# A decoder layer on one core: cross maximum subtracted by VectorE, one exp a block, and a new order of the scores

## What is computed

```python
def reference(x, ctx, w_qkv, b_qkv, w_proj, b_proj, w_q, w_k, w_v, w_o, k0, k1, k2, s0, s1, s2):
    x = layernorm(x + self_attention(x, w_qkv, b_qkv, w_proj, b_proj))     # causal
    # cross-attention
    q, k, v = heads(x @ w_q), heads(ctx @ w_k), heads(ctx @ w_v)
    attn = softmax(einsum('bhqd,bhkd->bhqk', q, k) * 64 ** -0.5)
    x = layernorm(x + merge(einsum('bhqk,bhkd->bhqd', attn, v)) @ w_o)
    h = relu(s0 * dense(k0, concatenate([x, -x]))) * 2
    h = relu(s1 * dense(k1, h)) * 2
    return layernorm(x + s2 * dense(k2, h))
```

## Time and profile before

| | |
|---|---|
| median of 3 runs | 2832.47 us (2832.13 to 2832.97) |
| the profiled execution | 2829.64 us, its span 2827.6 us |
| TensorE matmul busy | 2296.6 us (81% of the span) |
| VectorE busy | 1710.5 us (60%) |
| ScalarE busy | 1150.0 us (41%) |
| GpSimd busy | 720.4 us (25%) |
| mean granted clock of TensorE | 0.941 |

### The profile page before, as it was taken

How to read it: one execution, slowest core, us unless ns; L and a number is a source line. 1 busy time by engine, 2 the same in 40 slices (tenths; PEclk the granted TensorE clock), 3 DMA queues, 4 the chain that set the end, 5 groups by cost and what they waited for, 6 DMA issues and landing times. The chain is left out here.

```text
span 2827.6 us, 54422 instructions
## 1 busy us (share of the span) xinstructions
PE 2296.6 (81%) x18572; PEld 1931.4 (68%) x18572; DVE 1710.5 (60%) x4548; ACT 1150.0 (41%) x2568; POOL 720.4 (25%) x847
## 2 busy tenths in 40 slices
PE   8994688888888788888878788888878788888877
PEld 6883576766676666766667677766667666766666
DVE  4542566666666666666665566666665666666664
ACT  5552344443344334443344334444344334444332
POOL 1000222322322322232232322232232322232231
PEclk9996899999999999999999999999999999999999
DMA  8984322333321332333331232333332232233310
GB/s 265 293 265 95 52 41 51 60 60 60 56 55 46 52 56 34 60 60 60 60 56 48 46 56 34 60 60 60 60 56 47 47 56 38 55 60 60 60 31 12
DMA packets 205155, 196.57 MB, mean 70 GB/s; under 512 B 50130, under 2 KB 184306, under 8 KB 205042
## 3 DMA queue, kind: packets, MB, share of 16 engines
q1 hardware_dynamic: 205108, 195.94, 32.7%
HBM read 69.37 MB, written 58.87 MB: 45 GB/s over the span
## 5 line engine op out<-in xcount | busy, mean ns | idle before, releaser
L1180 PE MATMUL ps<-r_h,w 128*128 128x256 f16 x2048 | 511.6, 289 | 2.1 <-DVE r_l L806 2.0
L1181 PE MATMUL ps<-r_l,w 128*128 128x256 f16 x2048 | 508.9, 288 | 0.0
L821 DVE CUSTOM_DVE_ANT_0 junk<-ps,causal 128x128 bf16<-128x128 f32 (+1 forms) x1024 | 322.8, 353 | 196.5 <-PE ps L1212 188.4
L488 POOL TENSOR_TENSOR p<-p,inv 128x308 f32<-128x308 f32 x256 | 228.4, 899 | 612.1 <-DVE inv L872 612.1
L623 ACT ACTIVATE probs<-ps 128x768 f32<-128x768 f32 x256 | 207.7, 813 | 295.2 <-PE ps L1223 294.4
L598 ACT ACTIVATE p<-ps,low 128x77 f32<-128x77 f32 x1024 | 268.0, 409 | 97.0 <-DVE low L860 94.2
L1318 PE MATMUL ps<-vo_h,p2t 128*128 128x256 f32 (+1 forms) x1280 | 241.9, 291 | 50.9 <-DVE p2t L879 49.2
L475 POOL TENSOR_SCALAR_AFFINE_SELECT probs<-probs 128x512 f32<-128x512 f32 x256 | 164.1, 641 | 430.8 <-ACT probs L623 430.6
L806 DVE SCALAR_TENSOR_TENSOR r_l<-ps,r_h 128x512 f16<-128x512 f32 x256 | 175.7, 687 | 135.8 <-ACT r_h L563 135.7
L1180 PEld LDWEIGHTS ps<-r_h,w 128*128 128x128 f16 x2048 | 211.4, 103 | 55.7 <-issue 20.7
L1223 PE MATMUL ps<-q_st,k_bd 128*128 128x256 f32 x1024 | 180.8, 306 | 74.6 <-DMA q_st<-neg_max 61.0
(11 more groups left out here) (145 smaller groups left out, 5027.3 us busy)
## 6 DMA issues: line engine op xcount, KB each, us to landing
vo_scratch<-vo_out SPq DMA_DIRECT2D x80, 448.0 KB, 4.3
vo<-vo_scratch SPq DMA_DIRECT2D x64, 512.0 KB
q_st<-p2t SPq DMA_DIRECT2D x192, 128.0 KB
k_bd<-p2t SPq DMA_DIRECT2D x192, 128.0 KB, 6.6
q<-q SPq DMA_DIRECT2D x128, 128.0 KB, 2.1
k_bd<-k_scratch SPq DMA_DIRECT2D x64, 154.0 KB, 3.4
x_in<-in_x SPq DMA_DIRECT2D x32, 256.0 KB, 5.4
out<-y SPq DMA_DIRECT2D x32, 256.0 KB, 2.2
```

The costliest lines, as they stand in the source:

```text
L488: pool.tensor_tensor(heads, heads, inv.unsqueeze(3).to_broadcast([P, TB, 2, SK]), ALU.mult)\
L821: dve.tensor_tensor_reduce(out=junk[:, e, b * P:b * P + width], in0=ps[:, bank + b, e * width:(e + 1) * width], in1=causal[:, (1 - b) * P: ...
L1180: pe.matmul(dst, w1[:, kk, m * P:(m + 1) * P], r0_h[:, kk, :], start=kk == 0, stop=False)
L1181: last = pe.matmul(dst, w1[:, kk, m * P:(m + 1) * P], r0_l[:, kk, :], start=False, stop=kk == KF - 1)
```

## The change

In the cross softmax VectorE takes the maximum (`max2`; the sign of the scores is turned in the split of w_q) and, by a new instruction `cross_below`, subtracts it from the bank into a new tile `p2r` with four places. ScalarE makes one exp of 308 columns in place of four of 77, in place in `p2r`. The sum reads `p2r`, and GpSimd multiplies from `p2r` into `p2`. Scores t now wait for the subtraction t-2 (`d_b2`), and the subtraction t for the multiplication t-4.

The banks: all scores by query lie in banks 2 and 3, so that each pair waits for the row maxima of the pair before; the transposed probabilities lie in banks 1 and 7, the cross output in bank 6 alone, the transposes of x1 in bank 4. The rest is order.

```diff
         def self_bank(n):
-            return 6 if n in (3, 5) else 2
+        def p2t_bank(g, c):
+            return 7 if (3 * g + c) % 2 else 1
...
                 inverse_deviation(0, i)
+                pool.wait_ge(d_x1, nth(i, 2, 2))
                 for n, (rows, n0, n1) in enumerate(VO_CHUNKS):
...
-                act.wait_ge(d_m2, nth(i, KX, t + 1))
-                heads = unit_probs(t)
-                for j in range(4):
-                    last = act.activation(heads[:, j // 2, j % 2, :], ps[:, 4 + t % 2, j * SK:(j + 1) * SK], ACT.Exp,
-                                          bias=low2[:, t, j:j + 1], scale=-1.0)
-                last.then_inc(a_e2, 1)
+                act.wait_ge(d_b2, nth(i, KX, t + 1))
+                act.activation(p2r[:, t % 4], p2r[:, t % 4], ACT.Exp).then_inc(a_e2, 1)
...
             def attention(i, first, f, first_f=False, more=True):
-                for n in range(4):
+                for n in range(3):
                     self_probs(i, n)
                 negated_max(i, 1)
+                self_probs(i, 3)
+                if not first:
+                    transposed_x2(f)
                 self_probs(i, 4)
-                if not first:
-                    transposed_x2(f)
                 self_probs(i, 5)
...
+            def cross_below(i, t):
+
+                dve.wait_ge(d_m2, nth(i, KX, t + 1))
+                if t >= 4:
+                    dve.wait_ge(g_p2, nth(i, KX, t - 3))
+                dve.tensor_tensor(p2r[:, t % 4], ps[:, 4 + t % 2, 0:4 * SK].rearrange("p (j k) -> p j k", j=4),
+                                  max2[:, t, :].unsqueeze(2).to_broadcast([P, 4, SK]), ALU.subtract).then_inc(d_b2, 1)
...
-                dve.tensor_reduce(sum2[:, t, :].rearrange("p (b e) -> p b e", b=TB), unit_probs(t),
-                                  AX_X, ALU.add).then_inc(d_s2, 1)
+                dve.tensor_reduce(sum2[:, t, :], p2r[:, t % 4], AX_X, ALU.add).then_inc(d_s2, 1)
...
                 if t >= 2:
-                    pe.wait_ge(a_e2, nth(i, KX, t - 1))
+                    pe.wait_ge(d_b2, nth(i, KX, t - 1))
```

More of the change, by code:

```diff
@@ L912, in attention @@
                     self_values(i + 1)
+                if g is not None:
+                    ffn_norm(g)
                 dve.wait_ge(pe_pj, nth(i, 1, 1))
@@ L947, in attention @@
                 cross_probs_low(i, 0, 2)
-                for c in range(3):
-                    cross_probs_low(i, 1, c)
                 if more:
-                    self_max(i + 1, 2)
+                    self_max(i + 1, 4)
+                cross_probs_low(i, 1, 0)
+                cross_probs_low(i, 1, 1)
+                if not first:
+                    relu_low(0, r1_h, r1_l, a_r1, d_r1, f, 2)
+                cross_probs_low(i, 1, 2)
                 if not first:
@@ L1198, in transposed_x2, with scores_by_query @@
                 transposes(x2, 0, f, pe_x2t)
-            def scores_by_query(i, n, after_cross=True):
-                if n == 1:
-                    pe.wait_ge(d_mx, nth(i, 2 * H, 4))
-                if n == 3 and after_cross:
-                    pe.wait_ge(d_y2, nth(i, 1, 0))
-                if n == 2 and not after_cross:
-                    pe.wait_ge(d_mx, nth(i, 2 * H, 8))
-                if n >= 4:
-                    pe.wait_ge(d_mx, nth(i, 2 * H, 4 * n if n == 7 else 4 * (n - 1)))
-                bank = self_bank(n)
-                pe.matmul(ps[:, bank, 0:2 * P], q_st[:, n, 0:P], k_bd[:, n, :, 0:P], start=True, stop=True)
-                pe.matmul(ps[:, bank + 1, :], q_st[:, n, P:S], k_bd[:, n, :, :], start=True, stop=True)\
+            def scores_by_query(i, n):
+                if n >= 1:
+                    pe.wait_ge(d_mx, nth(i, 2 * H, 4 * n))
+                pe.matmul(ps[:, 2, 0:2 * P], q_st[:, n, 0:P], k_bd[:, n, :, 0:P], start=True, stop=True)
+                pe.matmul(ps[:, 3, :], q_st[:, n, P:S], k_bd[:, n, :, :], start=True, stop=True)\
                   .then_inc(pe_sq, 1)
@@ L1292, in cross_transposes @@
                     pe.wait_ge(g_p2, nth(i, KX, 4 * g + 4))
-                if unit == 0 and more:
-                    pe.wait_ge(d_mx, nth(i + 1, 2 * H, 8))
                 if unit >= 2:
@@ L1317, in cross_output @@
                         for b in range(TB):
-                            last = pe.matmul(ps[:, 6 + b, 0:D], p[0:rows, at, b * P:(b + 1) * P], w[0:rows, at, :],
-                                             start=g == 0 and n == 0 and k == 0, stop=g == 1 and n == VT - 1 and k == 2)
+                            last = pe.matmul(ps[:, 6, b * D:(b + 1) * D], p[0:rows, at, b * P:(b + 1) * P], w[0:rows, at, :],
+                                             start=g == 0 and n == 0 and k == 0 and b == 0,
+                                             stop=g == 1 and n == VT - 1 and k == 2 and b == TB - 1)
                 if g == 1 and c == 2:
@@ L1397, in attention @@
                 layer1_until(f, Z_PJ, Z_LN)
+                if more:
+                    pe.wait_ge(q_stacked, nth(i + 1, 112, 112))
+                    pe.wait_ge(k_stacked, nth(i + 1, 96, 96))
+                    scores_by_query(i + 1, 0)
                 pe.wait_ge(d_x1, nth(i, 2, 2))
-                transposes(x1, 3, i, pe_x1t)
+                transposes(x1, 4, i, pe_x1t)
                 layer1_until(f, Z_LN, Z_XT)
@@ L1406, in attention, with next_scores @@
                     pe.wait_ge(d_v, nth(i + 1, 1, 1))
+                def next_scores(n):
+                    if more:
+                        scores_by_query(i + 1, n)
                 cross_queries(i, 0)
+                next_scores(1)
                 cross_queries(i, 1)
```

127 lines of the change are left out of this document (55 added, 72 removed).

## The result

The changed kernel takes **2595.6 us** (median of 4 runs, 2594.1 to 2597.0) against 2832.3 us, a ratio of 0.917 with a 95% interval of 0.915 to 0.919. The forecast was 2621 us, faster, in a range of 2540 to 2730 us. The profiled execution took 2596.83 us with a span of 2594.7 us: 232.8 us less than the profiled one of before.

What follows compares the result with a forecast made beforehand. TensorE was taken as the bound. Per image -0.35 + 0.5 + 6.15 + 1.9 - 1.4 = 6.8 us, over 31 images 211 us, edges about 0, gave 2621 us with the median's 2.8 added; range 2540 to 2730 us.

Steps and rivals of the forecast that it cites:

- Stage (e): From the first head-stack DMA to the next x1 transposes: none of the 5.2 us gained, 1.4 us lost per image.
- Stage (c): The tail, from last cross scores to the next image's first scores by key: 24.65 to 18.5 us, gain 6.15.
- Stage (d): From the first scores by key to the first head-stack DMA: fewer TensorE waits, gain 1.9 us per image.
- Stage (b): The ring, from first to last of the eight cross scores: 11.39 to 10.9 us, gain 0.5 per image.
- Stage (a): From x1's transposes to the first cross scores: second scores by query now stand there, 0.35 us lost per image.
- Early stacks: Rival: head stacks land early, so VectorE's freed normalising sets the end of (e); 2429 us, chance 0.04.
- One pair of banks too few: Rival: later scores by query wait for row maxima, halving the gain of tail and (d); 2726 us, chance 0.13.
- GpSimd holding the ring: Rival: GpSimd's eight multiplications hold VectorE in the ring; slower, 2857 us at 7.6 us of holds, chance 0.04.
- No change: Rival: the tail's gain comes back as waits elsewhere, time within 0.2%; chance 0.04.

Runs made afterwards that it cites:

- no_hold: The changed kernel without GpSimd's new wait for the second x1; 2603.1 us, ratio 0.921 to the kernel before.
- gate_late_no_hold: The changed kernel with next-image scores and their stack wait moved behind the second cross queries (2363 us), then without GpSimd's wait for the second x1; 2546.5 us.
- bunched: The changed kernel with the next image's third to sixth scores by query put back together behind the last output piece; 2719.0 us, ratio 0.962 to before.
- old_exp: The changed kernel with the old softmax (minimum, four exps from the bank, no subtraction), keeping the contiguous tile; 2593.4 us, ratio 0.917 to before.
- before_hold: The kernel before with only GpSimd's wait for the second x1 added ahead of its vo_l subtraction; 2613.3 us, ratio 0.924 to before.

## Why the prediction was right, step by step

- **Stage (e), the step that mattered.** "Nothing of the 5.2 us of the held VectorE is gained" held: 0.74 us for the normalising, vo_l behind it, and TensorE's longest wait still there for another cause. no_hold and gate_late_no_hold show it from both sides, 8 and 183 us. The stage lost 1.86 us instead of 1.4: the stacks took 16.17 us in this image (1442.87 to 1459.04; 15.67 in the one before, 15.84 at the start), the scores 0.81 instead of 0.7.
- **Stage (c)** gave 5.93 of 6.15 us. Putting the middle scores back together undoes nearly all of it and half of the whole gain (bunched). The wait of 0.7 us at the second group's output was there (0.65): VectorE's low half, which it waits for, stands right behind row maxima 4 (1413.49 to 1414.85 us).
- **Stage (d)** gave 2.17 of 1.9. The waits that it named went, for x2's low half wholly and for the maxima's DMA all but 10.5 us; that ScalarE's order did it is argued, not tried.
- **Stage (b)** gave 0.58 of 0.5. The walk's own terms (3.6, 3.8, 2.4, 0.95) add up to 10.8 us, not 10.9, which is what was measured. The block was 1.28 us against 1.27; the subtraction 478 ns on average, 0.39 until the next starts; the sum 463 ns and 0.38. The forecast gave the one exp no value in time; old_exp agrees, and finds none for the subtraction either.
- **Stage (a)** lost 0.03 instead of 0.35 in the image read, and gained 0.28 over the 29 images. The second scores by query are there (pair 1 stands behind the first cross queries, so ahead of the ring and not in it), but the clock of the stage is 0.74 where it was 0.69.
- **The size.** 211 us was forecast and 237 measured. Over the 30 equal periods the gain was 7.35 instead of 6.8 us, 16 us in all; the last gained 14.3 instead of 13.4; start and end lost 2 instead of 6. Over the 29 images (b), (c) and (d) with (e) came within 0.1 us of the forecast; the term that was mis-sized is (a), by 0.6 us. The sum per image lies inside the bounds of 3.4 and 9.4 us that were given; how the upper one adds up from the terms named isn't shown. That the image read comes out at 72.06 us against 72.05 is in part luck: (a) was 0.3 us better and (e) 0.4 worse than forecast.
- **The rivals.** Early stacks: they didn't land early (15.67 and 16.17 us behind their first DMA). One pair of banks too few: scores by query waited 21.3 us in all for row maxima, 36 times, half of it in the first 300 us; behind that it is 0.4 us a time. The reason given against it was not right, though: between these rounds stand at most five filler quarters, not seven or more. GpSimd holding the ring: no subtraction took longer than 480 ns and no sum longer than 466, so nothing was held. No change: far off.
- **What the prediction left unsaid.** It counted the stall as unavoidable in this order, and it is. It didn't price the clock behind it apart, some 1.9 us an image here, and 2.15 in (a) of the kernel before. And the bare wait on GpSimd in the old order would have been worth 6.7 us an image: the new order spent that on the stacks, and earned 6.0 of its 7.4 us in the tail.

## What to carry to other kernels

When one wait ends a stage, write down the second one that would end it, with its time: here 0.56 us lay between them, so one line was worth 8 us or 183 us by what stood in front. A row that waits for a transfer belongs behind all work that doesn't need it, since the engine's order makes everything behind it wait too. And a stall has a second price in the clock of the matmuls after it; useless matmuls in a stall that can't be moved bought back 58 us.

## What was not expected of the hardware

- GpSimd's hold doesn't end with each of its instructions. In the kernel before, the first of VectorE's two normalising instructions ends at 1480.51 us, 0.15 us behind the first of the three subtractions; the second ends only behind the third, at 1484.08 us. In before_hold the first of y's pair starts in the second subtraction and takes 2.96 us, to 0.15 us behind the third:

```profile
1478.02 2.34 POOL L482 TENSOR_TENSOR vo_l<-vo,vo_h 128x1024 fp32r<-128x1024 f32 x1
```
```profile
1478.09 2.42 DVE L800 TENSOR_SCALAR x<-x,mv,rstd 128x256 f32<-128x256 f32 x1
```
```profile
1388.25 2.96 DVE L801 TENSOR_SCALAR y<-y,mv,rstd 128x256 f32<-128x256 f32 x1
```

The Trainium skill (SBUF — State Buffer, SBUF: two separate sides) says that whoever starts first keeps the shared pair for the whole instruction; the first two rows agree. Why VectorE gets in behind the first subtraction and not behind the second stays open.

- A sum over 308 contiguous columns takes 463 ns; the earlier trace rows has 0.72 and 0.76 us for the same count read with strides, although both lie in the same kind of memory.
- GpSimd's multiplication takes 0.78 us on average with a contiguous input (0.75 to 0.85 in the image read) and 0.90 on average in the kernel before (0.95 in the earlier trace rows), where it read and wrote the strided tile.
